# Reordering three TensorE transposes and their ScalarE copies at the head of each step of an audio tower block

## The reference, cut to what matters

```
x (32, 1024) -> patches of 16 -> xp (32, 64, 16), with a mask of ones beside it
h  = W_o @ silu(W_h @ [xp, mask] + b_h) + b_o + W_r @ [xp, mask] + b_r     # 512 hidden, 256 out
z  = layernorm(h)                                                          # per token, no affine
q, k, v = z per head (16 heads of 16) @ Wq.T, Wk.T, Wv.T
h  = h + softmax(q k^T / sqrt(256)) v @ W_out.T + b_out                    # over the 64 tokens of a sequence
z  = layernorm(h)
h  = h + real(ifft(fft(z) @ (w_real + i w_imag))) + bias                   # one real 256 x 256 matrix
```

## Time and profile before

| | us |
|---|---|
| median of 3 runs | 141.02 (140.94 to 141.13) |
| the profiled execution, its own time | 141.03 |
| its span, first to last instruction | 139.1 |
| TensorE busy in it | 132.8 (95%) |
| DVE busy | 111.8 (80%) |
| POOL busy | 94.7 (68%) |
| ScalarE (ACT) busy | 85.6 (62%) |

### The profile page before, as it was taken

How to read it: one execution, slowest core, us unless ns; L and a number is a source line. 1 busy time by engine, 2 the same in 40 slices (tenths; PEclk the granted TensorE clock), 3 DMA queues, 4 the chain that set the end, 5 groups by cost and what they waited for, 6 DMA issues and landing times.

```text
span 139.1 us, 6121 instructions
## 1 busy us (share of the span) xinstructions
PE 132.8 (95%) x2444; PEld 111.8 (80%) x2444; DVE 111.8 (80%) x337; ACT 85.6 (62%) x245; POOL 94.7 (68%) x186
## 2 busy tenths in 40 slices
PE   6979999999999998999999999999999999999991
PEld 2369999999997777978879889788798897887650
DVE  4574696959978587798898988988989889879671
ACT  5374765577878484956847649568476495663410
POOL 3285797997584455587687786876877868664750
PEclk9999999999999999999999999999999999999999
DMA  3678000031000010111302203123022031122012
GB/s 67 159 169 256 29 0 0 0 35 12 2 0 5 0 19 9 19 43 23 59 23 43 48 13 61 41 23 65 23 40 53 8 61 43 18 57 49 2 38 75
DMA packets 24509, 5.89 MB, mean 42 GB/s; under 512 B 20385, under 2 KB 24225, under 8 KB 24481
## 3 DMA queue, kind: packets, MB, share of 16 engines
q1 hardware_dynamic: 24192, 5.37, 18.4%
q10 hardware_dynamic: 288, 0.13, 0.4%
HBM read 2.35 MB, written 2.10 MB: 32 GB/s over the span
## 4 chain that ended last, share of the span: by engine, by line
PE 83%; DVE 6%; DMA 3%; issue 2%; POOL 1%; ACT 1%; SPq 1%; DVEq 0%
PE bank L1063 11%; PE bank L972 10%; PE bank L1049 7%; PE bank L1105 6%; PE bank L1125 6%; PE bank L977 5%; PE bank L1112 4%; PE bank L1158 4%; PE bank L1093 4%; DMA wf_raw<-in_W_r 3%; PE bank L1076 2%; PE bank L1171 2%; PE bank L966 2%; PE bank L1129 2%; PE bank L1162 2%
## 5 line engine op out<-in xcount | busy, mean ns | idle before, releaser
L829 DVE TENSOR_REDUCE bank<-bank 128x4 f32<-128x256 f32 x64 | 22.8, 425 | 6.8 <-ACT pT L378 6.4
L378 ACT ACTIVATE pT<-bank 128x256 f32<-128x256 f32 x64 | 19.4, 390 | 2.5 <-PE bank L1076 2.5
L1063 PEld LDWEIGHTS bank<-qT,xzT 32*128 32x128 f32 x512 | 15.7, 186 | 2.7 <-issue 2.7
L1063 PE MATMUL bank<-qT,xzT 32*128 32x64 f32 x512 | 17.9, 276 | 0.0
L700 DVE TENSOR_TENSOR hid_lo<-bank,hid_hi 128x512 fp32r<-128x512 f32 x16 | 11.0, 686 | 7.0 <-ACT bank L346 7.0
L587 POOL TENSOR_TENSOR side_lo<-sideT,side_hi 128x256 fp32r<-128x256 f32 x14 | 10.2, 727 | 8.3 <-ACT sideT L389 8.3
L373 ACT ACTIVATE maxT<-bank 128x128 fp32r<-128x128 f32 x16 | 4.4, 277 | 17.8 <-PE bank L1085 17.8
L548 POOL TENSOR_SCALAR xblk<-xh,parity_sb 128x128 f32<-128x128 f32 x32 | 11.5, 372 | 5.6 <-PE bank L1112 4.5
L598 POOL TENSOR_TENSOR on_lo<-onT,on_hi 128x256 fp32r<-128x256 f32 x14 | 10.3, 736 | 7.1 <-ACT on_hi L393 6.8
L556 POOL TENSOR_TENSOR hb_all<-h_all,bout_bc 128x256 f32<-128x256 f32 x16 | 11.5, 736 | 3.9 <-ACT h_all L350 3.9
L363 ACT ACTIVATE xzT<-bank,parity_sb 128x256 f32<-128x256 f32 x28 | 12.0, 497 | 0.0
(11 more groups left out here) (170 smaller groups left out, 386.8 us busy)
## 6 DMA issues: line engine op xcount, KB each, us to landing
out<-y SPq DMA_DIRECT2D x16, 128.0 KB, 1.7
xblk<-xh SPq DMA_DIRECT2D x32, 32.0 KB, 2.5
wo_raw<-in_W_o SPq DMA_DIRECT2D x1, 512.0 KB, 4.2
wout_raw<-in_W_out SPq DMA_DIRECT2D x1, 256.0 KB, 3.8
fr<-in_wr SPq DMA_DIRECT2D x1, 256.0 KB, 4.3
fi<-in_wi SPq DMA_DIRECT2D x1, 256.0 KB, 4.4
minus_raw<-in_minus_rows SPq DMA_DIRECT2D x1, 128.0 KB, 2.5
bout_bc<-in_b_out SPq DMA_DIRECT2D x1, 128.0 KB, 4.0
```

Source lines behind the costliest of these rows:

```text
L378: nc.scalar.activation(pT[:, j, :], bank[j][:, D:2 * D], ACT.Exp).then_inc(exp_done, 1)
L829: nc.vector.tensor_reduce(rowmax[:, j, :], bank[j][:, 0:D].rearrange("p (h k) -> p h k", k=TOK), AX_X, ALU.max).then_inc(max_done, 1)
L1063: pe.matmul(bank[j][:, at0:at0 + TOK], xzT[t % 3][rows32, 2 * half + b, :, :].rearrange("p e k -> p (e k)"), qT[t % 3][rows32, half, TOK * ...
```

## The change

In TensorE's `step`, `turn_x` is moved from behind to ahead of the two other turns. In ScalarE's `step`, `copy_xT` is moved from behind to ahead of `copy_max` and `copy_side`; `copy_xzT` stays where it was. Nothing is added or removed, and the code of POOL, DVE and SyncE is the same.

```
             def step(i):                      # ScalarE
+                if i + 3 < T:
+                    copy_xT(i + 3)
                 if i + 1 < T:
                     copy_max(i + 1)
                 if i >= 1:
                     copy_side(i - 1)
                 if i + 3 < T:
-                    copy_xT(i + 3)
                     copy_xzT(i + 3)

             def step(i):                      # TensorE
                 if 0 <= i + 2 < T:
                     scores_inputs(i + 2)
+                if 3 <= i + 3 < T:
+                    turn_x(i + 3)
                 if i >= 1:
                     turn_side(i - 1)
                 if 0 <= i + 1 < T:
                     turn_max(i + 1)
-                if 3 <= i + 3 < T:
-                    turn_x(i + 3)
                 if 0 <= i + 2 < T:
                     scores(i + 2)
```

## The result

| | us |
|---|---|
| before, median of 5 runs | 141.02 (140.8 to 141.13) |
| after, median of 5 runs | 145.14 (144.96 to 145.35) |
| ratio | 1.0295, 95% interval 1.028 to 1.0309 |
| span of the profiled execution, before and after | 139.1 and 143.1 |

The kernel became slower by 4.1 us, where 2.5 were forecast; the time lies 0.7 us above the range. The direction and the mechanism hold, one term of the sum does not. First the page after: busy time by engine, the granted clock, and the shares of the chain that ended last.

The account below looks back on a forecast made before the run. TensorE's list was taken to bound a step at 5.56 us; after the change a ring through ScalarE and POOL, 5.81. Ten rounds of 0.25 add 2.5 to 141.03, giving 143.5 us, range 142.6 to 144.4.

Parts of the forecast that it names:

- the first part: Kernel before: TensorE's list sets the step, 5.56 us until step 12; xh comes 0.06 us before its use.
- The ring: TensorE's turns, ScalarE's copies, POOL's list to xh, next turn of x: 5.81 us a step, 0.25 more than TensorE's list.
- point 2: Feedback through TensorE, ScalarE and POOL sums to 5.81 us a step against TensorE's 5.56 and becomes the bound.
- point 1: TensorE's turn of x in first place waits for POOL's xh, 0.29 us without feedback; side rows and maxima queue behind.
- term (f): From the end of POOL's xh to TensorE's next turn of x: 0.06 us, upper bound 0.12.
- point 3: ScalarE's earlier x_hi takes 0.26 us off the way to on_hi, eaten by the maxima turned 0.22 us later.
- point 4: Other waits do not bind; xh's DMA copies land at 103.4 to 104.6, before L580 overwrites the buffer at 104.78.
- point 5: Step 1 gains 0.22 us, used up at step 2; ten rounds from step 2 to 12 cost 2.5 us.
- dearer: Rival: the sum's upper bounds together, each link adding some hundredths at its wait, 144.5 to 145.0; chance 7%.
- The clock: Rival: TensorE's idle 0.25 us before transposes in each of ten steps lowers its clock, 146 or above; chance 2%.

Follow-up runs that it names:

- e6: Kernel before, with POOL's normalisation that makes xh moved ahead of the bias sum h2b: 144.79 us, ratio 1.0294.
- e3: Kernel before, with ScalarE's order alone changed (copy_xT ahead of copy_max), TensorE's list untouched: 142.91 us, ratio 1.0143.
- e4: Kernel before, with TensorE's order alone changed (turn_x ahead of the other turns), ScalarE's list untouched: 147.77 us, ratio 1.0487.
- e5: Changed kernel, with POOL's normalisation that makes xh moved ahead of the bias sum h2b: 145.92 us, ratio 1.0368.
- e1: Changed kernel, with TensorE's wait for xh_set coded first, so that it is checked last before the first transpose: 143.18 us, ratio 1.0163.
- e2: Changed kernel, with two already satisfied waits added before the first transpose, one more semaphore instruction after xh's arrival: 145.94 us, ratio 1.0362.
- e7: Kernel before, with both engines' new order in steps 0 and 1 only: 140.47 us over 10 runs, ratio 0.9976.

## Why the prediction was right and wrong

- *TensorE bounds a step, xh comes just in time* (the first part): right. TensorE's own list is 5.56 us, shown by e6's steps 2 and 3.
- *The ring through ScalarE and POOL becomes the bound* (point 2): right, link by link up to xh. Shown by the links' positions in the profile after, by e3 and e4, which shift its parts, and by e5's first two steps, where it is open and the loss is gone.
- *The latency from xh to the turn* (point 1 and term (f)): **the step that failed.** I took 0.06 us and 0.12 as its upper bound; it is 0.226. 0.166 more in each of ten rounds is 1.66 us, and 143.5 + 1.66 = 145.16, against 145.14 measured. I took the value from rows in which the late wait sits on the transpose's own weight load. The nearest row was the earlier trace rows, where the late wait (h2) shares a semaphore instruction with another and the load follows: 0.12. The lists in the section on the change even show the three semaphores on the transpose, with xh_set first. I read them for what is waited for and not for the order, and bounded the cost with a row that has one semaphore instruction too few between. e1 and e2 show the price from both sides. The range was also cut short: it ended at 144.4, although the prediction's own bounds reached 145.0.
- *ScalarE's move helps by 0.26* (point 3): right, 6.25 us without it (e4), 5.98 with it.
- *The DMA copies land in time* (point 4): right for this change. How near they are, e5 and e6 show: 0.73 us earlier is too early for xh.
- *Step 1 gives and step 2 takes back, ten rounds* (point 5): ten rounds is right. That step 2 starts within 0.02 us of the forecast, once the first parts are laid over each other, is luck. Two misses of the same size cancel there. Step 0 gives too, which the prediction left out: the gain is 0.39 us and not 0.22, and xh of tile 5 ends at 60.18 + 0.19 = 60.37 where 60.55 was forecast. The latency that follows it is 0.17 longer. The latency thus stands in eleven turns, that of step 2 among them, and only because step 0 pays for that one do ten make up the difference. e7 shows the gain by itself.
- The rival "dearer" (144.5 to 145.0) comes nearest, by a sum that did not happen. It had 0.06 more in (f) and 0.03 to 0.1 before maxT; maxT came at 0.80 as in the forecast, and (f) alone brought 0.166. The clock did not fall: 1.000 in the profile after, and 0.997 in e4, whose idle time before the turn (0.73) is three times that forecast; the kernel before has 0.996 to 1.000 in its own executions. So the Trainium skill's remark on transposes (TensorE: Matmul & The Clock Gate, the part on transposes) had no consequence here.

## What to carry to other kernels

When a wait moves to another instruction, look at which waits it then shares that instruction with, and in what order they are checked: what becomes ready last should be checked last. And when an in-order engine is the bound with a just-in-time input, follow that input back to the engine: if the way back begins with the reordered work, the cost is the length of the ring less the engine's own step, in every round. In this kernel the reordering gained only in the rounds in which the engine idled anyway (steps 0 and 1), and made there alone it was worth 0.3 us (e7).

## What the runs showed of the hardware

Waits that are already satisfied are not free behind a late one. On TensorE one semaphore instruction took 0.11 us from start to start and the weight load followed the last by 0.08, in every round from step 2 on: 0.05 us from the end of xh to the load with none between (e1), 0.23 with two instructions (after, e4), 0.33 with three (e2). The Trainium skill (Perfetto Trace Analysis, Identifying Dependency Chains) says that an instruction which waits for several engines may have semaphore instructions with further conditions put ahead of it; the records agree, and add the price. The timeline hints at it: the idle time before the turn is put down to "issue" in the changed kernel and to "POOL xh" in e1, where xh's wait is the last. The kernel before had the same pair: "issue" in the earlier trace rows, with 0.12 us, and "DVE h" in the earlier trace rows, with 0.06.
